# Six plain norms of the joined feed-forward and projection stage on Pool, with the pieces of the stage in another order

## The chip, the cores and the metric

One core of a Trainium2 chip runs the whole kernel as one program. TensorE multiplies and transposes (PE in the profile), VectorE is DVE, ScalarE is ACT, GpSimd is Pool (POOL); SyncE (SP) starts the DMAs. Each engine works through its own list of instructions in order, and they meet only at semaphores. The metric is the time of one execution on the device in microseconds (us), as the median of several runs; lower is better.

## The reference, cut to what matters

```python
x = x + _L0_xattn_ref(_layernorm(x), ctx_512, ctx_512, ...)   # 16 heads, keys and values from ctx_512
x = x + _L0_ffn_ref(_layernorm(x), w_gate, w_up, w_down)      # ternary feed-forward, 8-bit activations
x = x + _L1_xattn_ref(_layernorm(x), ctx_512, ...)            # LN, self-attention + FF, LN, cross-attention + FF
x = x + _L1_ffn_ref(_layernorm(x), W1, W2, Wg, bg)            # one of 8 experts per token

def _bitlinear(x, w):                  # the ternary layers
    return jnp.einsum('bsi,oi->bso', _act_quant(x), _weight_quant(w))
gate = jax.nn.silu(_bitlinear(x, w_gate)); up = _bitlinear(x, w_up)
return _bitlinear(gate * up, w_down)

# L1: x = _ln(xx, ln1_g, ln1_b); then q, k, v from _ln(x, ...) for 16 heads of 32, S = 256, width 256
```

x has the shape (8, 256, 256), f32. `_act_quant` scales each row by its largest absolute value to 127 and rounds. "Plain" norm means (x - mean) / sqrt(var + eps) without gain and bias.

## The kernel before, in words

The 2048 rows of x are cut into 16 tiles of 128 rows; NP = 4 "pairs" p of 4 tiles each (512 rows) are the unit in which most pieces work, X[p] holds a pair, Y[p] the input of the second block. The program has six stages: first cross-attention ("L0", to about 135 us), the joined stage (to about 306 us), self-attention a1, its feed-forward, cross-attention a2, experts.

The joined stage does two things for each pair, one pair behind the other. First the ternary feed-forward: `attended_sum` adds the attention's output to X[p]; `front_stats` (bn_stats, bn_aggr), then `front_apply` writes the plain norm of X[p] to XHB; `front_scales` and `front_quant` quantize it to N1 (bf16 integers) and `input_transposes`/`input_copy` turn it into N1T. For each tile i of the pair, `gate_up(p, i, j)` multiplies by half j of both weights, `silu` (ScalarE) and `gated` (VectorE) form the hidden row tile HH, `hidden_quant` quantizes it, `whole` (ScalarE) makes bf16 integers, `hidden_transposes`, `whole_copy`, `down` and `down_sum` bring the result into X[p]. Then the input of the second attention: `output_stats`, `gain` and `bias` (a norm with gain and bias, to Y[p]), `normed_stats`, and `second_norm` writes the plain norm of Y[p] to XHC; `a1_transposes`, `a1_input(p, "x")` and `a1_input(p, "y")` (ScalarE) and 12 pieces `project(p, k)` with `project_copy` follow, four each for queries, keys and values.

The reciprocal roots of all norms are made by Pool: `rstd` waits for the variance (`var_ready`), adds eps, takes the power -0.5 and signals `rstd_ready`. The statistics lie in a ring of four places in `small`, and Pool takes them strictly in the order in which VectorE makes them. In the joined stage Pool has nothing else.

The order of the pieces is written out by hand, one call after the other, for each of VectorE, ScalarE and TensorE. A piece waits by semaphore for what it needs. Between neighbours that matter here: `gate_up` of tile g waits for `gated` of tile g-1, half j (the PSUM bank); `hidden_transposes` of tile g for `whole_copy` of tile g-1; `down` of g for `down_sum` of g-1; `a1_transposes(p)` for the norm in XHC and for the 12th `project_copy` of the pair before; `gain(p)` writes into XHC and waits for the transposes of pair p-1; `a1_transposes(0)` also waits for `attended_sum(3)`.

In lines of the profile: L714 `apply` (all plain norms on VectorE), L871 the largest value in `quant_scales`, L878 `attended_sum`, L896 and L898 `front_quant`, L905 `gated`, L913 `hidden_quant`, L917 `down_sum`, L698 and L701 statistics, L722 `gain`, L729 `bias`; TensorE: L1648 transposes of f32 rows, L1904 `input_transposes`, L1915 `gate_up`, L1931 `hidden_transposes`, L1940 `down`, L2003 and L2005 `project`; ScalarE: L1356 `input_copy`, L1364 `silu`, L1369 `whole`, L1376 `whole_copy`, L1382 `a1_input`, L1395 `project_copy`; Pool: L488 to L492 `rstd`.

Of the kernel before, what the change touches and what calls it, by code (L numbers as in the profile page):

```python
# [48 lines left out]
def build(nc, ins, out):  # L49
    ctx = ExitStack()  # L50
    with ctx:
# [239 lines left out]
        def first_weights(b):  # L291
# [75 lines left out]
        with nc.Block() as block:  # L367
# [125 lines left out]


# [189 lines left out]
            def _(dve):  # L684
# [266 lines left out]
                kf1 = front_stats(1)  # L951
# [6 lines left out]
                hidden_quant(0, 0)  # L958
# [49 lines left out]
                gated(2, 2, 0)
                bias(1, ko1)
                gated(2, 2, 1)  # L1010
                kn1 = normed_stats(1)
                hidden_quant(2, 2)
                second_norm(1, kn1)
# [1421 lines left out]
```

## Time and profile before

| | before |
|---|---|
| runs | 1103.16 us median (1101.93 to 1103.17, 3 runs) |
| the execution under the profile | 1102.89 us, span 1101.1 us |
| TensorE matmuls busy | 1032.0 us, 94% of the span |
| VectorE busy | 535.5 us, 49% |
| ScalarE busy | 465.4 us, 42% |
| Pool busy | 268.5 us, 24% |
| mean granted TensorE clock | 0.994 of full |

Busy shares are of the whole span, and its stages have different limits, so a change in one stage is read from the stretch of that stage and from the waits in it. A row of the timeline gives the start, the length from the first start to the last end, the engine and line, the output and inputs, the count of instructions merged, and in brackets how long the engine was idle before it and what ended that.

### The profile page before, as it was taken

What the parts mean: (1) busy time and instruction counts of PE and PEld (TensorE: products, weight loads), DVE (VectorE), ACT (ScalarE), POOL (GpSimd) and SP (SyncE); (2) the same over time, 40 slices, a digit from 0 to 9 for tenths busy, and PEclk for the clock granted to TensorE, in tenths of its full rate; (3) what the DMA queues carried; (4) which work ended last, traced back from release to release, by engine and by line L of the source; (5) the groups of instructions that cost most, each with busy time, mean ns of one, the idle gap of its engine ahead of it and who ended that gap; (6) DMA issues with size and microseconds to landing.
All of it is one profiled execution on the core that took longest, in us unless ns stands there. A gap on an engine that the chain in (4) does not pass through costs nothing.

```text
span 1101.1 us, 20861 instructions
## 1 busy us (share of the span) xinstructions
PE 1032.0 (94%) x8679; PEld 740.4 (67%) x8679; DVE 535.5 (49%) x1293; ACT 465.4 (42%) x715; POOL 268.5 (24%) x409
## 2 busy tenths in 40 slices
PE   7998877999989999999999999999999999999997
PEld 4655544555467777776676475667578658999996
DVE  5577789985257788741531333775332233200000
ACT  6767565665455555552222325554311231122220
POOL 3023201101023334332212111556320102322211
PEclk9999999999999999999999999999999999999999
DMA  8600000000060000000000020000710217755410
GB/s 256 90 2 1 2 1 1 1 1 0 1 153 2 2 3 2 2 1 1 1 1 0 1 96 1 3 2 2 229 39 21 95 46 271 282 190 189 161 51 1
DMA packets 55359, 60.56 MB, mean 55 GB/s; under 512 B 23603, under 2 KB 47071, under 8 KB 55266
## 3 DMA queue, kind: packets, MB, share of 16 engines
q1 hardware_dynamic: 52322, 52.93, 15.7%
q0 software_dynamic: 2944, 6.30, 1.9%
q8 instruction: 69, 1.13, 0.4%
q14 instruction: 24, 0.20, 0.1%
HBM read 54.76 MB, written 7.21 MB: 56 GB/s over the span
## 4 chain that ended last, share of the span: by engine, by line
PE 72%; DVE 19%; ACT 3%; issue 2%; DMA 1%; POOL 1%; SPq 1%; DVEq 0%; POOLq 0%; ACTq 0%
PE ps L1879 15%; PE ps L2179 10%; DVE small L790 9%; PE ps L2321 8%; PE ps L2334 7%; PE ps L1739 6%; PE ps L2003 3%; PE ps L1710 3%; PE ps L2254 3%; PE ps L1792 2%; PE ps L1730 2%; PE ps L1707 2%; PE ps L1648 2%; PE ps L2005 1%; DVE small L871 1%
## 5 line engine op out<-in xcount | busy, mean ns | idle before, releaser
L790 DVE TENSOR_REDUCE small<-ps 128x4 f32<-128x1024 f32 (+2 forms) x112 | 145.4, 1334 | 74.8 <-PE ps L1710 60.0
L1879 PE MATMUL ps<-r_w,r_k 128*128 128x256 f32 x512 | 113.2, 381 | 2.5 <-ACT r_k L1549 2.5
L2179 PE MATMUL ps<-r_a,r_w 128*128 128x512 f32 x256 | 112.1, 594 | 3.1 <-ACT r_a L1382 3.1
L1879 PEld LDWEIGHTS ps<-r_w,r_k 128*128 128x128 f32 x512 | 96.4, 190 | 18.6 <-issue 4.4
L1792 PE MATMUL ps<-r_a,onesf 128*32 128x256 f32 (+1 forms) x768 | 84.3, 387 | 8.3 <-ACT r_a L1302 8.3
L2179 PEld LDWEIGHTS ps<-r_a,r_w 128*128 128x128 f32 x256 | 48.2, 190 | 60.2 <-issue 56.0
L2321 PE MATMUL ps<-r_a,w_block 128*128 128x128 f32 x736 | 86.4, 275 | 1.0 <-ACT r_a L1610 1.0
L2321 PEld LDWEIGHTS ps<-r_a,w_block 128*128 128x128 f32 x736 | 85.6, 192 | 2.5 <-ACT r_a L1610 1.0
L1549 ACT ACTIVATE r_k<-ps,pvec 128x512 f32<-128x512 f32 x64 | 44.0, 687 | 100.6 <-PE ps L2179 100.6
L1302 ACT ACTIVATE r_a<-ps 120x1024 f32<-120x1024 f32 (+1 forms) x64 | 65.5, 1024 | 43.5 <-PE ps L1746 43.2
L2334 PE MATMUL ps<-w_all,r_a 128*128 x368 | 83.2, 379 | 0.2 <-issue 0.2
L1618 ACT ACTIVATE r_a<-ps 128x512 f32<-128x512 f32 x46 | 27.5, 597 | 129.3 <-PE ps L2321 115.8
L578 POOL TENSOR_SCALAR_AFFINE_SELECT r_a<-r_a 128x256 f32<-128x256 f32 x128 | 47.5, 407 | 120.8 <-ACT r_a L1302 120.8
L1313 ACT ACTIVATE r_a<-ps 128x512 f32<-128x512 f32 (+1 forms) x64 | 45.0, 704 | 69.9 <-PE ps L1799 50.0
L2334 PEld LDWEIGHTS ps<-w_all,r_a 128*128 128x128 f32 x368 | 68.2, 190 | 8.7 <-issue 0.3
L1305 ACT ACTIVATE r_a<-ps 120x512 f32<-120x512 f32 (+1 forms) x128 | 69.4, 596 | 6.4 <-PE ps L1746 6.4
L1746 PE MATMUL ps<-maxT,sel 32*120 32x256 f32 (+1 forms) x512 | 65.2, 363 | 2.4 <-ACT maxT L1295 2.4
L491 POOL TENSOR_TENSOR small<-small,epst 128x4 f32<-128x4 f32 (+2 forms) x31 | 6.2, 199 | 224.8 <-DVE small L701 224.5
L2003 PE MATMUL ps<-r_a,r_w 128*128 128x512 f32 x128 | 58.7, 597 | 1.5 <-issue 0.9
L1382 ACT ACTIVATE r_a<-ps,pvec 128x512 f32<-128x512 f32 x40 | 28.6, 775 | 71.3 <-PE ps L1648 66.7
L1879 PE MATMUL ps<-r_w,r_q 128*128 128x256 f32 x256 | 57.0, 380 | 0.1
L1792 PEld LDWEIGHTS ps<-r_a,onesf 128*32 128x32 f32 (+1 forms) x768 | 31.2, 108 | 32.1 <-ACT r_a L1302 14.6
(265 smaller groups left out, 1816.7 us busy)
## 6 DMA issues: line engine op xcount, KB each, us to landing
w_block<-in_L_ffn_W SPq DMA_DIRECT2D x23, 1024.0 KB
w_all<-in_L_ffn_W SPq DMA_DIRECT2D x8, 1024.0 KB, 9.4
r_w<-in_L_xattn_a_li_w SPq DMA_DIRECT2D x4, 1024.0 KB, 7.3
x_rows<-x_all SPq DMA_DIRECT2D x4, 512.0 KB, 3.0
x_rows<-r_a SPq DMA_DIRECT2D x4, 512.0 KB, 3.0
x_all<-in_x SPq DMA_DIRECT2D x3, 512.0 KB, 5.8
y_all<-in_L_ffn_w_gate SPq DMA_DIRECT2D x1, 1024.0 KB, 8.8
y_all<-in_L_ffn_w_up SPq DMA_DIRECT2D x1, 1024.0 KB, 11.3
```

The lines of the kernel that those rows point to most:

```text
L578: ins_ = pool.affine_select(out=PM[:, 2 * h:2 * h + 2, x, :], in_=PT[:, 2 * h:2 * h + 2, q0:q0 + P], compare_op=ALU.is_gt, fill=0.0, base= ...
L790: ins_ = dve.tensor_reduce(nm.rearrange("p (j s) -> p j s", j=4)[:, j:j + count, :], src, AX.X, ALU.max, negate=True)
L1302: act.activation(PT[0:nk, 0:2, :], bank(n % 2, 0, 2)[0:nk], ACT.Exp, scale=scale).then_inc(sem["exp_done"], 1)
L1305: act.activation(PT[0:nk, 2:4, S * x:S * (x + 1)], bank(n % 2, 2, 2)[0:nk, :, S * x:S * (x + 1)], ACT.Exp, scale=scale).then_inc(sem["exp_ ...
L1739: pe.matmul(bank(n % 2, j)[0:nk, column(None, x)], keys(n, j, x), queries(n, j, x), start=(x == 0), stop=False, tile_position=(32 * j, 0))
L1746: ins_ = pe.matmul(bank(n % 2, j)[0:nk, column(None, x)], sel[32 * j:32 * j + 32, 0 if UNIT_OF[n][0] == "a1" else x, 0:nk], maxT[32 * j:32 ...
L1792: pe.matmul(bank(n % 2, 1)[32 * j:32 * j + 32, at:at + S], ones, weights_of(n, j, x), start=(a == "a2" or x == 0), stop=(a == "a2" or x == ...
L1879: ins_ = pe.matmul(o[:, t // 2, (t % 2) * D:(t % 2 + 1) * D], src[:, c, t * P:(t + 1) * P], w[:, c, :], start=(c == 0), stop=(c == chunks ...
L2003: ins_ = pe.matmul(o, w[:, c, m * P:(m + 1) * P], x[:, c, :], start=(c == 0), stop=(c == KC - 1))
L2179: ins_ = pe.matmul(o, LI[a]["li2"][:, c, m * P:(m + 1) * P], FT3[:, c, :], start=(c == 0), stop=(c == KC - 1))
L2321: ins_ = pe.matmul(ps[:, 2 * (b % 2) + h, m * P:(m + 1) * P], W1B[w][:, c, (4 * h + m) * P:(4 * h + m + 1) * P], FB[b % 2][:, c, :], start ...
L2334: ins_ = pe.matmul(ps[:, 4 + b % 2, 0:D], HB[b % 2][:, c, :], W2A[:, bass.ds(e, 1), c, :].rearrange("p o n -> p (o n)"), start=(c == 0), s ...
```

## The change

Six applications of a plain norm move from VectorE to Pool: `front_apply` for pairs 1, 2 and 3 and `second_norm` for pairs 0, 1 and 2. `front_apply(0)` and `second_norm(3)` stay on VectorE. Pool's new code (new lines, with the roots around it):

```diff
+                def normalise(dst, src):
+                    at = LN_W * ((norms - 1) % 4)
+                    pool.wait_ge(sem["rstd_ready"], norms)
+                    for t in range(PT_TILES):
+                        ins_ = pool.tensor_scalar(dst[:, t, :], src[:, t, :], sa(at + 48 + 2 * t, 1), sa(at + 72 + t, 1), ALU.subtract, ALU.mult)
+                    return ins_
+                def front_apply(p):
+                    pool.wait_ge(sem["n1_ready"], p)
+                    normalise(XHB, X[p]).then_inc(sem["front_ready"], 1)
+                def second_norm(p):
+                    normalise(XHC, Y[p]).then_inc(sem["c_xh_ready"], 1)
...
                 rstd()
+                front_apply(1)
                 rstd()
+                front_apply(2)
                 rstd(twice=True)
                 rstd()
+                second_norm(0)
                 rstd()
+                front_apply(3)
                 rstd(twice=True)
                 rstd()
+                second_norm(1)
                 rstd(twice=True)
                 rstd()
+                second_norm(2)
...
                 def front_scales(p):
+                    if p >= 1:
+                        dve.wait_ge(sem["front_ready"], p)
...
-                gated(0, 0, 0)
-                front_apply(1, kf1)
+                hidden_quant(0, 0)
                 front_scales(1)
```

The rest is the order of the calls, on VectorE, ScalarE and TensorE. `hidden_quant` of tile (0, 0) comes before the feed-forward scales of pair 1; `attended_sum(3)` comes behind `normed_stats(0)` and `hidden_quant(1, 1)`; `front_scales(3)` and `front_quant(3)` come before `output_stats(1)`. On TensorE each `hidden_transposes` and `down` of the middle of the stage stands somewhat earlier among the gate_up and project pieces, `input_transposes(1)` stands before `down(0, 1)`, and at the end the first scores of a1 come before `project(3, 4)` and `project(3, 5)` and not behind them. On ScalarE a `whole` is moved in between `a1_input(0, "x")` and `a1_input(0, "y")`, and `whole(3, 2)` stands earlier among the project copies, further ahead of `a1_input(2, "x")`. Nothing is computed otherwise and no DMA moves.

VectorE, from the gain of pair 0 to the first `hidden_quant` behind it. Before (L878 is `attended_sum(3)`, the two L714 are `second_norm(0)` and `front_apply(2)`):

```order
L722 SCALAR_TENSOR_TENSOR r_a<-x_all,small,bvec 128x256 x4
L905 SCALAR_TENSOR_TENSOR r_a<-ps,small,r_a 128x512
L729 SCALAR_TENSOR_TENSOR y_all<-r_a,small,bvec 128x256 x4
L905 SCALAR_TENSOR_TENSOR r_a<-ps,small,r_a 128x512
L698 BN_STATS small<-y_all 128x6 x4
L701 BN_AGGR small<-small 128x2 x4
L878 TENSOR_TENSOR x_all<-ps,x_all 128x1024
L714 TENSOR_SCALAR r_a<-y_all,small 128x256 x4
L905 SCALAR_TENSOR_TENSOR r_a<-ps,small,r_a 128x512
L714 TENSOR_SCALAR r_a<-x_all,small 128x256 x4
L871 TENSOR_REDUCE small<-r_a 128x1
```

The same place on VectorE afterwards (lines are about 22 to 24 higher: L744 is gain, L751 bias, L929 gated, L893 to L937 `hidden_quant`, L900 `attended_sum(3)`):

```order
L744 SCALAR_TENSOR_TENSOR r_a<-x_all,small,bvec 128x256 x4
L751 SCALAR_TENSOR_TENSOR y_all<-r_a,small,bvec 128x256 x4
L929 SCALAR_TENSOR_TENSOR r_a<-ps,small,r_a 128x512
L720 BN_STATS small<-y_all 128x6 x4
L723 BN_AGGR small<-small 128x2 x4
L893 TENSOR_REDUCE small<-r_a 128x1
L894 TENSOR_SCALAR small<-small 128x1
L895 RECIPROCAL small<-small 128x1
L936 TENSOR_SCALAR small<-small,mean_w 128x1
L937 TENSOR_SCALAR r_a<-r_a,small 128x1024
L900 TENSOR_TENSOR x_all<-ps,x_all 128x1024
L929 SCALAR_TENSOR_TENSOR r_a<-ps,small,r_a 128x512 x2
```

Both norms are gone from VectorE, one gated half-tile has moved behind, and `hidden_quant(1, 1)` has moved ahead of `attended_sum(3)`.

TensorE around the first a1 transposes. Before (L1879 is `output(3)`, L1648 the a1 transposes of pair 0, L2003 `project(0, 0)`):

```order
L1879 MATMUL ps<-r_w,r_v 128x256 x8
L1915 MATMUL ps<-r_k,r_a 128x512 x16
L1931 MATMUL ps<-identb,r_a 128x128 x8
L1648 MATMUL ps<-ident,r_a 128x128 x8
L1915 MATMUL ps<-r_k,r_a 128x512 x4
L1940 MATMUL ps<-r_v,r_a 128x256 x8
L2003 MATMUL ps<-r_a,r_w 128x512 x2
```

TensorE at the same place afterwards (L1897 `output(3)`, L1958 `down`, L1933 `gate_up`, L1949 `hidden_transposes`, L1666 a1 transposes, L2021 `project(0, 0)`):

```order
L1897 MATMUL ps<-r_w,r_v 128x256 x8
L1958 MATMUL ps<-r_v,r_a 128x256 x8
L1933 MATMUL ps<-r_k,r_a 128x512 x4
L1949 MATMUL ps<-identb,r_a 128x128 x8
L1666 MATMUL ps<-ident,r_a 128x128 x8
L1933 MATMUL ps<-r_k,r_a 128x512 x8
L1958 MATMUL ps<-r_v,r_a 128x256 x8
L1949 MATMUL ps<-identb,r_a 128x128 x8
L2021 MATMUL ps<-r_a,r_w 128x512 x2
```

The hidden transposes right ahead of the a1 transposes are now those of tile (1, 1) and no longer of (1, 0), and one more down and one more hidden transpose stand ahead of `project(0, 0)`.

Pool from the root of `front_stats(2)` on, before:

```order
L491 TENSOR_TENSOR small<-small,epst 128x4
L492 TENSOR_TENSOR small<-small,neghalf 128x4
L488 TENSOR_TENSOR small<-small,onepe 128x4
L489 TENSOR_TENSOR small<-small,eps 128x4
L492 TENSOR_TENSOR small<-small,neghalf 128x4
```

Pool at the same place afterwards:

```order
L491 TENSOR_TENSOR small<-small,epst 128x4
L492 TENSOR_TENSOR small<-small,neghalf 128x4
L499 TENSOR_SCALAR r_a<-x_all,small 128x256 x4
L488 TENSOR_TENSOR small<-small,onepe 128x4
L489 TENSOR_TENSOR small<-small,eps 128x4
L492 TENSOR_TENSOR small<-small,neghalf 128x4
L491 TENSOR_TENSOR small<-small,epst 128x4
L492 TENSOR_TENSOR small<-small,neghalf 128x4
L499 TENSOR_SCALAR r_a<-y_all,small 128x256 x4
```

Each moved norm stands right behind the root that it uses and ahead of the next root.

## Rows read from the trace of the kernel before

**Rows 1.** Stretches: busy us (instructions) of the five engines, granted clock, DMA share, GB/s.
```profile
174.00:186.00 12.00, 7.12 (x37) 4.25 (x36) 11.61 (x30) 5.64 (x10) 1.21 (x2) 0.86 0.00 1
...
139.00:225.00 86.00, 72.00 (x403) 42.17 (x402) 81.92 (x204) 52.83 (x71) 8.05 (x15) 0.96 0.00 1
225.00:306.00 81.00, 79.68 (x293) 38.50 (x290) 40.12 (x100) 41.85 (x64) 5.69 (x10) 1.00 0.00 1
```

**Rows 2.** Timeline of TensorE, 140 to 306 us: start, length, work, idle before.
```profile
180.57 1.97 PE L1648 MATMUL ps<-ident,r_a 128*128 128x128 f32 x8 [3.02 <-DVE r_a L714]
...
185.50 1.96 PE L2003 MATMUL ps<-r_a,r_w 128*128 128x512 f32 x4 [0.53 <-ACT r_a L1382]
...
191.23 0.61 PE L1931 MATMUL ps<-identb,r_a 128*128 128x128 bf16 x8
191.68 1.04 PE L1940 MATMUL ps<-r_v,r_a 128*128 128x256 bf16 x8
193.05 0.61 PE L1904 MATMUL ps<-identb,r_a 128*128 128x128 bf16 x8 [0.33 <-ACT r_a L1376]
...
220.08 1.07 PE L1648 MATMUL ps<-ident,r_a 128*128 128x128 f32 x8
...
223.72 0.62 PE L1904 MATMUL ps<-identb,r_a 128*128 128x128 bf16 x8 [0.84 <-DVE r_a L898]
...
254.18 1.07 PE L1648 MATMUL ps<-ident,r_a 128*128 128x128 f32 x8
...
259.39 7.11 PE L2003 MATMUL ps<-r_a,r_w 128*128 128x512 f32 x16 [0.93 <-issue]
...
281.16 1.09 PE L1648 MATMUL ps<-ident,r_a 128*128 128x128 f32 x8 [0.39 <-DVE r_a L714]
```

**Rows 3.** Timeline of VectorE in the joined stage.
```profile
139.92 1.37 DVE L714 TENSOR_SCALAR r_a<-x_all,small 128x256 f32<-128x256 f32 x4
...
145.25 1.21 DVE L871 TENSOR_REDUCE small<-r_a 128x1 f32<-128x1024 f32 x1
...
147.67 1.22 DVE L878 TENSOR_TENSOR x_all<-ps,x_all 128x1024 f32<-128x1024 f32 x1
...
159.59 0.48 DVE L917 SCALAR_TENSOR_TENSOR x_all<-ps,small,x_all 128x256 f32<-128x256 f32 x1 [1.06 <-PE ps L1940]
...
177.79 1.23 DVE L878 TENSOR_TENSOR x_all<-ps,x_all 128x1024 f32<-128x1024 f32 x1
...
180.43 0.74 DVE L905 SCALAR_TENSOR_TENSOR r_a<-ps,small,r_a 128x512 f32<-128x512 f32 x1
181.09 1.37 DVE L714 TENSOR_SCALAR r_a<-x_all,small 128x256 f32<-128x256 f32 x4
...
215.78 1.19 DVE L871 TENSOR_REDUCE small<-r_a 128x1 f32<-128x1024 f32 x1
...
219.87 1.21 DVE L871 TENSOR_REDUCE small<-r_a 128x4 f32<-128x1024 f32 x1
...
250.27 1.38 DVE L714 TENSOR_SCALAR r_a<-y_all,small 128x256 f32<-128x256 f32 x4 [1.40 <-POOL small L492]
```

**Rows 4.** Timeline of ScalarE in the joined stage.
```profile
139.91 0.69 ACT L1364 ACTIVATE r_a<-ps,small 128x512 f32<-128x512 f32 x1 [0.69 <-PE ps L1915]
...
172.90 1.14 ACT L1369 ACTIVATE r_a<-r_a,neg_magic 128x1024 bf16<-128x1024 f32 x1
...
182.58 2.78 ACT L1382 ACTIVATE r_a<-ps,pvec 128x512 f32<-128x512 f32 x4 [2.81 <-PE ps L1648]
```

**Rows 5.** Pool's groups by shape: busy us, mean ns, idle before.
```profile
L578 POOL TENSOR_SCALAR_AFFINE_SELECT r_a<-r_a 128x256 f32<-128x256 f32 x128 | 47.5, 407 | 120.8 <-ACT r_a L1302 120.8
...
L585 POOL TENSOR_TENSOR y_all<-y_all,bvec 128x256 f32<-128x256 f32 x32 | 23.9, 747 | 16.2 <-DVE max_rows L796 16.2
```

**Rows 6.** Timeline of all engines, 104 to 106 us.
```profile
104.76 1.19 DVE L868 TENSOR_SCALAR r_k<-r_k 128x2048 f32<-128x2048 f32 x1
104.92 1.62 POOL L542 TENSOR_TENSOR r_v<-r_a 128x256 f32<-128x256 f32 x1 [4.70 <-DVE r_a L820]
```

More of the change, by code:

```diff
@@ L978, in _ @@
                 gain(0, ko0)
+                bias(0, ko0)
                 gated(1, 1, 1)
-                bias(0, ko0)
+                normed_stats(0)
+                hidden_quant(1, 1)
+                attended_sum(3)
                 gated(1, 2, 0)
-                kn0 = normed_stats(0)
-                attended_sum(3)
-                second_norm(0, kn0)
                 gated(1, 2, 1)
-                front_apply(2, kf2)
-                hidden_quant(1, 1)
+                hidden_quant(1, 2)
                 down_sum(1, 0)
-                hidden_quant(1, 2)
                 front_scales(2)
@@ L995, in _ @@
                 hidden_quant(1, 3)
-                kf3 = front_stats(3)
                 gated(2, 0, 0)
+                front_stats(3)
                 gated(2, 0, 1)
-                front_apply(3, kf3)
+                gated(2, 1, 0)
                 hidden_quant(2, 0)
-                gated(2, 1, 0)
                 gated(2, 1, 1)
+                hidden_quant(2, 1)
                 down_sum(1, 2)
-                hidden_quant(2, 1)
+                front_scales(3)
+                gated(2, 2, 0)
+                front_quant(3)
+                gated(2, 2, 1)
                 down_sum(1, 3)
                 ko1 = output_stats(1)
+                hidden_quant(2, 2)
                 gain(1, ko1)
-                gated(2, 2, 0)
                 bias(1, ko1)
[L1010 to L1013, printed above, removed]
+                normed_stats(1)
                 down_sum(2, 0)
-                front_scales(3)
-                front_quant(3)
-                down_sum(2, 1)
                 gated(2, 3, 0)
@@ L1020, in _ @@
                 hidden_quant(2, 3)
-                down_sum(2, 2)
+                down_sum(2, 1)
                 gated(3, 0, 0)
                 gated(3, 0, 1)
+                down_sum(2, 2)
                 hidden_quant(3, 0)
-                down_sum(2, 3)
                 gated(3, 1, 0)
                 gated(3, 1, 1)
+                gated(3, 2, 0)
                 hidden_quant(3, 1)
+                down_sum(2, 3)
                 ko2 = output_stats(2)
-                gated(3, 2, 0)
+                gated(3, 2, 1)
                 gain(2, ko2)
+                hidden_quant(3, 2)
                 bias(2, ko2)
-                kn2 = normed_stats(2)
-                second_norm(2, kn2)
-                gated(3, 2, 1)
-                hidden_quant(3, 2)
+                normed_stats(2)
                 down_sum(3, 0)
@@ L2137, in _ @@
                 scores(FIRST["a1"])
+                project(3, 4)
+                project(3, 5)
                 project(3, 6)
```

165 lines of the change are left out of this document (81 added, 84 removed).

## The prediction

> **What bounds the kernel now.** The run under the profile took 1102.89 us around a span of 1101.1 us, so 1.8 us lie outside the span; the median of the runs is 1103.16 us, 0.27 us above the profiled run. I add up against 1102.89. A measurement of this kernel can tell about 0.2%, 2.2 us, from no change.
>
> I looked first at the busy time by stretch. The edit reaches only the joined stage, about 135 to 306 us, and this stage has two halves with different limits [rows 1]. From 139 to 225 us VectorE is busy 81.9 of 86 us and TensorE 72.0. From 225 to 306 us TensorE is busy 79.7 of 81 us and VectorE 40.1. So VectorE sets the pace first and TensorE afterwards. Work taken off VectorE counts only in the first half, and only if TensorE has something to do with the time.
>
> Then the timeline of TensorE with the idle time before each piece, to see what a gain can be made of [rows 2]: 3.02 us before the transposes of the first second-attention input at 180.57, 0.53 at 185.50, 0.33 at 193.05, 0.84 at 223.72, 0.93 at 259.39, 0.39 at 281.16. The second half has almost nothing to win: from 225 us on it is a queue of matmuls, and it ends when they are done. The stage gets shorter by as much idle (and slow) TensorE time as goes away, not by as much as VectorE is relieved.
>
> There is slow time too: in the stretch 174 to 186 us the granted clock is 0.86 on average [rows 1]. The f32 transposes at 180.57, after 3.02 us of idle, take 1.97 us, the same eight at 281.16 take 1.09 [rows 2]. A long wait costs TensorE nearly 1 us again behind it.
>
> **The change, part by part.**
>
> *Off VectorE.* Six norms of four instructions. The row at 139.92 is 1.37 us, the last at 250.27 is 1.38 [rows 3], so 6 x 1.37 = 8.2 us. The last of the six stands where TensorE is the limit and hides its absence: 5 x 1.37 = 6.9 us is all that VectorE can give, and an upper end for the gain from this part.
>
> *Onto Pool.* 24 instructions that subtract and multiply, 128x256. No row shows that on Pool. The nearest from below is the one-input select of the same size, 0.41 us; from above the two-input add, 0.75 us [rows 5]. The new one reads one big input as the select does, so I take 0.45 to 0.5 each, 2.0 us for four, with 1.6 to 3.0 as the bounds. On VectorE it was 1.37 us, so the result of a norm comes later than before, counted from its statistics: 1.40 us for the root on Pool (the wait of VectorE before 250.27 [rows 3]) plus 2.0 instead of 1.4.
> The three norms of the feed-forward input have slack: norm 1 is ready at about 141 and is wanted only after hidden_quant(0, 0), at about 143.7; norms 2 and 3 are ready long before. I cost them at nothing, hidden by hidden_quant and its neighbours. The three for the second attention are not hidden: a1_transposes waits for them.
> The same Pool queue holds every reciprocal root. Behind front_apply(2) stands the root of output_stats(0), some 6 us later; no root comes within 2 us of a moved norm.
>
> *The first half, rewalked.* hidden_quant takes 147.67 - 145.25 = 2.42 us from start to start; one half-tile of gated takes 181.09 - 180.43 = 0.66 [rows 3]. In the old order the sum attended_sum(3) starts at 177.79. In the new one front_apply(1) is gone (-1.4, start to start), gated(1, 2, 0) stands behind (-0.66), hidden_quant(1, 1) ahead of it (+2.42). gated(0, 0, 1) finds its ScalarE piece (139.91 to 140.60 [rows 4]) unready and waits some 0.7 us that front_apply(1) used to cover; of the 1.06 us wait at 159.59 [rows 3] about 0.6 goes, since quantization 1 is earlier but down(0, 1) now stands behind input_transposes(1). Sum: 177.8 - 1.4 - 0.7 + 2.4 + 0.7 - 0.6 = 178.2 us.
> TensorE now has hidden_transposes(1, 1) in front of the a1 transposes. They need hidden_quant(1, 1), done at 178.3, and ScalarE's copy of it, 1.14 us [rows 4]: 179.5 us. So TensorE idles longer than before, about 4.5 us (from 175 on), and runs slowly again: the hidden transposes some 0.9 us, twice their 0.45 (below), the a1 transposes from 180.4 with 1.97 us, to 182.4. At full clock it would be 180.0 and 181.1. Then ScalarE makes both inputs (2.78 us, row 182.58) with one whole copy of 1.14 between them [rows 4], 3.9 us: project(0, 0) starts between 185.0 and 186.3; I take 186.1. Before it is 185.50 [rows 2], so **0.6 us is lost** here. But by then three more pieces are done than before: down(1, 1), hidden_transposes(1, 1) and hidden_transposes(1, 2). Start to start a hidden transpose is 191.68 - 191.23 = 0.45 us, a down 193.05 - 0.33 - 191.68 = 1.04 [rows 2]; I take 0.9 for the down, since its end overlaps the next piece. That is 1.8 us of work. **Ahead by 1.2 us.**
>
> *From there on.* VectorE has no second_norm and front_apply any more, and front_scales(3) and front_quant(3) stand before output_stats(1), so N1 for input 3 is there long before TensorE asks. The waits of 0.33 and 0.84 us go. The 0.93 us before 259.39 is project(2, 0) waiting for ScalarE's inputs [rows 2]; whole(3, 2) no longer stands before those on ScalarE, so it goes too. **+2.1 us.**
> Is Pool on time here? For norm 1, VectorE needed 215.78 - 177.79 = 38.0 us from attended_sum(3) to the end of normed_stats(1). Now three norms are missing there (-4.1), gated(1, 2, 0) is in (+0.7), front_scales(3) and front_quant(3) are in (+3.8, from 219.87 [rows 3] to the transposes released at 223.72 [rows 2]): 178.2 + 38.0 + 0.4 = 216.6. XHC is there at 216.6 + 1.4 + 2.0 = 220.0. TensorE took 220.08 - 185.50 = 34.6 us from project(0, 0) to a1_transposes(1) [rows 2]; now gate_up(2, 3, 1) and input_transposes(3) come before it, 0.9 + 0.5, two hidden transposes and the 0.33 wait are gone, -1.2: 186.1 + 34.8 = 220.9. On time with 0.9 us of slack. For norm 2, gate_up(3, 2, 1) ends at about 238.5, and gated, gain, hidden_quant(3, 2), bias and statistics follow it on VectorE, 0.7 + 1.7 + 2.4 + 1.7 + 1.8 = 8.3: 246.8, with a wait for ScalarE 247.5; XHC at 250.9. TensorE's place is 254.18 [rows 2] less what is gained by then, 1.2 + 0.33 + 0.84: 251.8, slack 0.9 again. These slacks are of the size of my errors, so I take off **0.3 us** for them. The last norm stays on VectorE, and its 0.39 us wait stays.
>
> *The scores before project(3, 4).* Nothing: max_transposes stands behind project(3, 11) either way, and what follows it waits for ScalarE's last project_copy and the table load behind that.
>
> Sum: 1.2 + 2.1 - 0.3 = 3.0 us. 1102.89 - 3.0 = **1099.9 us**.
>
> **A row and a rule that speak against it.** Pool and VectorE disturb each other in this trace. Pool's multiply at 104.92 took 1.62 us, where the add of the same size takes 0.75, and VectorE's one-input 128x2048 instruction ran from 104.76 for 1.19 us [rows 5, 6]: 0.9 us lost by Pool. A moved norm meets about one such VectorE instruction, the scaling in hidden_quant, shorter than that one: an estimated loss of up to 0.7 us, within the slack of each norm that TensorE waits for.
> The Trainium skill, "SBUF — State Buffer", section "Who interferes with whom", says that the port pair shared by VectorE and GpSimd is an exclusive lock, and that whoever issues second is blocked for the whole instruction. By that VectorE would lose too, when Pool is first. The row shows only Pool's loss; no row before shows VectorE's.
>
> **The rivals.**
> 1. *VectorE is held up by Pool.* Each of the five norms of the first half makes VectorE wait once or twice for one Pool instruction of 0.45 us, 2.3 to 4.5 us in the half where VectorE is the limit. For it: VectorE is 95% busy there, so hardly a Pool instruction runs beside idle. Against: most of what VectorE does is reductions, statistics and PSUM reads, and its one disturbed neighbour in the trace was Pool. At 2.3 us the gain is 0.7 us: 1102.2.
> 2. *Pool is too slow, and the a1 transposes wait for it: slower.* With x us more per norm than the 2.0 assumed, the first transposes are late by x - 1.2 (XHC at 178.2 - 2.4 + 1.4 + 2.0 = 179.2 against 180.4), the other two by x - 0.9 each. At 0.75 a piece (x = 1.0) that is 0.2, still 1100.1. The whole gain is gone at 3x - 3.0 = 3.0, x = 2.0 or 1.0 us a piece, and it is slower by 0.2% from x = 2.7, 1.18 us a piece. At 1.3 (x = 3.2) 6.6 us are lost: 1106.5. For it: the 1.62 us row. Against: that row is one in several, and 24 pieces would have to be hit.
> 3. *The order is better than my walk.* If TensorE does not slow down after its wait and Pool is on time, the 0.6 loss and the 0.3 go and about 1 us of slow time too: gain 4.9, 1098.0.
> 4. *Nothing of it reaches the end*: the norms move as said, but the chain down, statistics, gain, bias, norm, transposes, ScalarE inputs sets project(0, 0) and then a1 transposes 1 to 3, as it did; 1102.9.
>
> **How the numbers follow.** The forecast with its own range, 1098.6 to 1101.6, has 0.54; rival 1 0.14, rival 2 0.12, rival 3 0.11, rival 4 0.09. Of the forecast's 0.54 some 0.42 lies above a gain of 2.2 us. Faster: 0.42 + 0.11 = 0.53. Slower: 0.09 of rival 2, and 0.04 from rival 1 at its upper end and from a chain that I misread, 0.13. Same: the rest, 0.34. The range goes from rival 3 with a little more, 1097.4, over rivals 1 and 4 and the milder half of rival 2, to 1104.0.
>
> **What the profile after would show.** Pool: 24 new instructions at 0.4 to 0.55 us; more than 0.9 is rival 2. VectorE: the 128x1024 scaling in hidden_quant and the 128x256 in front_quant keep the same duration everywhere; if some are 0.4 us longer, rival 1. TensorE: an idle of 4 to 5 us before the hidden transposes at about 179 us, project(0, 0) at 185 to 186.5, hardly any idle from there to the a1 transposes of pair 3, and those at about 278 instead of 281.16. After 306 us everything is the same and only earlier. I would be wrong if TensorE idles again between 186 and 250 us, which would mean that VectorE or ScalarE is late where I found slack of only 1 to 2 us (gate_up(2, 1, 1), down(1, 3)).

## The result, and the profile after

| | before | after |
|---|---|---|
| median of the runs | 1103.16 us (1101.93 to 1103.58, 6 runs) | 1109.31 us (1107.04 to 1111.48, 6 runs) |
| the execution under the profile | 1102.89 us, span 1101.1 | 1111.48 us, span 1109.8 |
| TensorE matmuls busy | 1032.0 us | 1038.7 us |
| VectorE busy | 535.5 us | 527.9 us |
| Pool busy | 268.5 us | 298.8 us |

The ratio is 1.0052, 95% interval 1.004 to 1.0064: slower by 6 us (0.5%) where 3 us less was forecast. The profiled execution is the longest of the six, so the trace shows 8.7 us of span where the medians show 6.2.

First, where the time is. The stretch from 139 us to the first transposes of the a1 maxima (305.78 before, 314.50 after), and the rest; columns as in [rows 1]. Before:

```profile
139.00:305.78 166.78, 151.46 (x692) 80.53 (x691) 122.04 (x304) 94.65 (x132) 13.74 (x25) 0.98 0.00 1
305.78:1100.00 794.22, 761.25 (x6621) 581.12 (x6619) 323.15 (x791) 278.41 (x449) 219.34 (x319) 1.00 0.20 64
```

After, with the stretch of the first a1 transposes on top:

```profile
174.00:186.00 12.00, 5.33 (x31) 3.72 (x31) 11.69 (x27) 2.86 (x3) 6.16 (x6) 0.73 0.00 1
...
139.00:314.50 175.50, 157.05 (x693) 84.54 (x691) 114.62 (x280) 95.94 (x132) 43.97 (x49) 0.93 0.00 1
314.50:1109.00 794.50, 761.20 (x6621) 581.07 (x6619) 323.04 (x791) 278.41 (x449) 219.67 (x319) 1.00 0.20 64
```

Behind the stage both kernels have the same busy times. In it the same matmuls (692 and 693 records) take 8.7 us more: 5.6 us more busy time of TensorE, since the mean granted clock is 0.93 and not 0.98, and 3.1 us more idle (175.50 - 157.05 = 18.45 against 15.32). Some 1 us of the slow time lies at the very start, ahead of any wait for Pool: from 139 to 143 us the clock is 0.62 after and 0.94 before. That need not come from the change: e1 and e7 below, which keep TensorE's old order, have 0.68 and 0.55 there. VectorE has 7.4 us less to do and nothing comes of it.

The timeline of TensorE after, at the places of [rows 2]:

```profile
181.35 1.04 PE L1949 MATMUL ps<-identb,r_a 128*128 128x128 bf16 x8 [4.43 <-ACT r_a L1387]
184.02 1.97 PE L1666 MATMUL ps<-ident,r_a 128*128 128x128 f32 x8 [1.64 <-POOL r_a L499]
185.79 3.62 PE L1933 MATMUL ps<-r_k,r_a 128*128 128x512 bf16 x8
...
190.84 1.94 PE L2021 MATMUL ps<-r_a,r_w 128*128 128x512 f32 x4
192.61 0.61 PE L1922 MATMUL ps<-identb,r_a 128*128 128x128 bf16 x8
...
194.83 1.89 PE L1933 MATMUL ps<-r_k,r_a 128*128 128x512 bf16 x8
...
228.36 1.97 PE L1666 MATMUL ps<-ident,r_a 128*128 128x128 f32 x8 [2.98 <-POOL r_a L499]
230.12 1.91 PE L1958 MATMUL ps<-r_v,r_a 128*128 128x256 bf16 x8
...
264.13 1.09 PE L1666 MATMUL ps<-ident,r_a 128*128 128x128 f32 x8 [1.80 <-POOL r_a L499]
...
268.14 7.11 PE L2021 MATMUL ps<-r_a,r_w 128*128 128x512 f32 x16
...
289.88 1.09 PE L1666 MATMUL ps<-ident,r_a 128*128 128x128 f32 x8 [0.42 <-DVE r_a L736]
```

Each of the three a1 transposes whose norm went to Pool now ends a wait for Pool: 1.64, 2.98 and 1.80 us, 6.4 together. Behind the first two TensorE runs near the lower of its two clocks, 1.2 of 2.4 GHz (granted 0.54 from 181 to 190.5 us and 0.56 from 228 to 235): eight gate_up matmuls at 185.79 take 3.62 us, eight of the same at 194.83 take 1.89. The waits of 0.33, 0.84 and 0.93 of [rows 2] are gone (192.61 and 268.14 have none). The last a1 transposes stand at 289.88, not 281.16; this start is the mark that I compare below. A mark is from one execution, and executions scatter: those of the kernel before lie between 1101.5 and 1106.3 us, and e1, whose time equals that kernel's and whose only edit lies on Pool, has the mark at 282.32. I take a difference of less than about 1 us at the mark as not shown.

Pool's norms, first in the timeline and then as groups (busy us, mean ns of one):

```profile
139.54 4.86 POOL L499 TENSOR_SCALAR r_a<-x_all,small 128x256 f32<-128x256 f32 x4 [0.20 <-POOL small L492]
...
179.02 4.95 POOL L499 TENSOR_SCALAR r_a<-y_all,small 128x256 f32<-128x256 f32 x4
...
223.04 5.26 POOL L499 TENSOR_SCALAR r_a<-y_all,small 128x256 f32<-128x256 f32 x4
...
259.24 4.84 POOL L499 TENSOR_SCALAR r_a<-y_all,small 128x256 f32<-128x256 f32 x4
```

```profile
L499 POOL TENSOR_SCALAR r_a<-x_all,small 128x256 f32<-128x256 f32 x12 | 15.2, 1275 | 0.5 <-POOL small L492 0.5
L499 POOL TENSOR_SCALAR r_a<-y_all,small 128x256 f32<-128x256 f32 x12 | 15.1, 1267 | 0.3
```

1.27 us a piece, where the forecast took 0.45 to 0.5.

### The profile page after: what moved, and what is told of

It is laid out like the page before. It is cut to its first block, busy times and chain, and to the rows that moved or that the text cites. A ratio compares the mean times of both kernels' runs of the same rounds, so it can differ in the third digit from the quotient of the medians.

```text
span 1109.8 us, 20862 instructions
## 1 busy us (share of the span) xinstructions
PE 1038.7 (94%) x8679; PEld 744.9 (67%) x8679; DVE 527.9 (48%) x1269; ACT 466.2 (42%) x715; POOL 298.8 (27%) x433
## 4 chain that ended last, share of the span: by engine, by line
PE 72%; DVE 18%; ACT 3%; POOL 3%; issue 2%; DMA 1%; SPq 1%; DVEq 0%; POOLq 0%; ACTq 0%
PE ps L1897 15%; PE ps L2197 10%; DVE small L812 9%; PE ps L2339 7%; PE ps L2352 7%; PE ps L1757 6%; PE ps L1728 3%; PE ps L2021 3%; PE ps L2272 2%; PE ps L1810 2%; PE ps L1748 2%; PE ps L1666 2%; PE ps L1725 2%; PE ps L1933 1%; POOL r_a L499 1%
## 5 line engine op out<-in xcount | busy, mean ns | idle before, releaser
L1897 PE MATMUL ps<-r_w,r_k 128*128 128x256 f32 x512 | 113.2, 381 | 2.5 <-ACT r_k L1567 2.5
L1897 PEld LDWEIGHTS ps<-r_w,r_k 128*128 128x128 f32 x512 | 96.4, 190 | 18.6 <-issue 4.4
L2021 PE MATMUL ps<-r_a,r_w 128*128 128x512 f32 x128 | 57.8, 596 | 0.0
L1897 PE MATMUL ps<-r_w,r_q 128*128 128x256 f32 x256 | 57.1, 380 | 0.1
```

The source lines that it names most:

```text
L1897: ins_ = pe.matmul(o[:, t // 2, (t % 2) * D:(t % 2 + 1) * D], src[:, c, t * P:(t + 1) * P], w[:, c, :], start=(c == 0), stop=(c == chunks ...
L2021: ins_ = pe.matmul(o, w[:, c, m * P:(m + 1) * P], x[:, c, :], start=(c == 0), stop=(c == KC - 1))
```

## The experiments

Three theories stood at the start. P: the form of Pool's instruction is dear in itself, and what follows is lateness at the a1 transposes. L: Pool and VectorE lock each other out, which makes both slow. O: the new order of the pieces is worse, whoever makes the norms. "The mark" is the start of the a1 transposes of pair 3.

| kernel | order | feed-forward norms 1 to 3 | second norms 0 to 2 | median us | ratio to before (95%) | mark |
|---|---|---|---|---|---|---|
| before | old | VectorE | VectorE | 1103.2 to 1103.7 | 1 | 281.16 |
| after | new | Pool | Pool | 1109.3 | 1.0052 (1.004, 1.0064) | 289.88 |
| e2_cheap | new | left out | left out | 1102.0 | 0.9985 (0.9975, 0.9994) | 279.77 |
| e3_order_only | new | VectorE | VectorE | 1106.5 | 1.0027 (1.0018, 1.0037) | 286.18 |
| e4_norms_only | old | Pool | Pool | 1115.3 | 1.0102 (1.0085, 1.0119) | 293.51 |
| e5_fronts_pool | new | Pool | VectorE | 1103.9 | 1.0002 (0.9993, 1.0011) | 282.43 |
| e8_split | new | Pool | 2 tiles each | 1105.6 | 1.0019 (1.001, 1.0028) | 283.45 |
| e6_double_second | new | Pool | Pool, twice | 1127.3 | 1.0216 (1.0201, 1.0232) | 308.02 |
| e7_old_fronts23 | old | 2, 3 on Pool | VectorE | 1102.8 | 0.9998 (0.9989, 1.0007) | 280.76 |
| e9_hybrid_cheap | old, then new | left out | left out | 1105.0 | 1.0007 (0.9998, 1.0015) | 282.61 |
| e10_hybrid_fronts | old, then new | 2, 3 on Pool | VectorE | 1107.2 | 1.0028 (1.0019, 1.0038) | 285.14 |
| e11_swap | new, one place changed | Pool | VectorE | 1103.4 | 1.0004 (0.9994, 1.0013) | 281.97 |

### e1: what a piece costs on Pool

Before, with instructions on Pool added behind the root at 139 us that write to unused space (twelve, where the expectation says 14; the last three repeat the second to the fourth):

```diff
+ pool.tensor_scalar(po[:, 0, :], bvec[:, 1, :], m_, r_, ALU.subtract, ALU.mult)
+ pool.tensor_scalar(po[:, 1, :], bvec[:, 1, :], m_, None, ALU.subtract)
+ pool.tensor_scalar(po[:, 2, :], bvec[:, 1, :], 0.5, 2.0, ALU.subtract, ALU.mult)
+ pool.tensor_scalar(po[:, 3, :], bvec[:, 1, :], 0.5, None, ALU.subtract)
+ pool.tensor_copy(po[:, 4, :], bvec[:, 1, :])
+ pool.tensor_tensor(po[:, 5, :], bvec[:, 1, :], m_.to_broadcast([P, D]), ALU.subtract)
+ link(pool.tensor_scalar(po[:, 6:8, :], bvec[:, 1:3, :], m_, r_, ALU.subtract, ALU.mult))
+ link(pool.tensor_scalar(po[:, 0:4, :], bvec[:, 1:5, :], m_, r_, ALU.subtract, ALU.mult))
+ pool.tensor_scalar(po[:, 0, :], bvec[:, 1, :], m_, r_, ALU.subtract, ALU.mult)
...
```

> The old kernel with 14 extra Pool instructions in the 24 us in which Pool is idle after the first root of the joined stage; their results are used by nobody. They are the norm's own form (two per-partition scalars) at 256, 512 and 1024 elements, the same with one per-partition scalar, with two constants, with one constant, a copy, and a two-input subtract with a broadcast. Theory P (the form is dear on Pool): the norm's form takes about 1.2 us at 256 elements, every time, and grows in proportion (2.4 at 512, 4.8 at 1024), and one of the other forms is much cheaper. Theory L (the form is cheap, but Pool is locked out by VectorE): its shortest instance is near 0.5 us and the instances scatter. Which of P's causes it is (per-partition scalars or two operations) shows in the variants: with constants about 0.5 if the scalars are the cause, with one scalar about 0.7 if it is the number of operations. The kernel's time should stay within 1 us of before.

The kernel took 1103.22 us. Timeline of its Pool, in the order of the edit:

```profile
139.30 1.24 POOL L564 TENSOR_SCALAR r_a<-bvec,small 128x256 f32<-128x256 f32 x1
140.54 0.92 POOL L565 TENSOR_SCALAR r_a<-bvec,small 128x256 f32<-128x256 f32 x1
141.44 1.14 POOL L566 TENSOR_SCALAR r_a<-bvec 128x256 f32<-128x256 f32 x1
142.55 0.85 POOL L567 TENSOR_SCALAR r_a<-bvec 128x256 f32<-128x256 f32 x1
143.35 0.39 POOL L568 COPY r_a<-bvec 128x256 f32<-128x256 f32 x1
143.73 0.61 POOL L569 TENSOR_TENSOR r_a<-bvec,small 128x256 f32<-128x256 f32 x1
144.34 2.07 POOL L570 TENSOR_SCALAR r_a<-bvec,small 128x512 f32<-128x512 f32 x1
146.51 3.78 POOL L571 TENSOR_SCALAR r_a<-bvec,small 128x1024 f32<-128x1024 f32 x1
150.39 1.22 POOL L572 TENSOR_SCALAR r_a<-bvec,small 128x256 f32<-128x256 f32 x1
151.59 1.26 POOL L573 TENSOR_SCALAR r_a<-bvec,small 128x256 f32<-128x256 f32 x1
```

VectorE in the same stretch:

```profile
139.92 0.75 DVE L919 SCALAR_TENSOR_TENSOR r_a<-ps,small,r_a 128x512 f32<-128x512 f32 x1 [1.99 <-ACT r_a L1378]
140.58 1.74 DVE L728 TENSOR_SCALAR r_a<-x_all,small 128x256 f32<-128x256 f32 x4
```

The form itself costs 1.22 to 1.24 us. With constants for the two operands it is 1.14, with one operation and a constant 0.85, while a copy of the same size takes 0.39 and a subtraction with two inputs 0.61. From 512 to 1024 elements 1.71 us are added, 3.3 ns an element, less than the proportion that was expected (2.07 us at 512, where 2.4 was expected). The piece at 139.30 took 1.24 us although VectorE was idle until 139.92, and at 150.39, beside other work of VectorE, it is 1.22 again, so P holds for the price. What is left of L is small and goes both ways. VectorE's norm at 140.58, beside three of these, took 1.74 us where it takes 1.37 in [rows 3]. And the form with one operation and its operand from SBUF took 0.92 us at 140.54 but 1.26 at 151.59, where VectorE's scaling in hidden_quant (151.78, 0.82 us instead of 0.74) ran beside it.

### e2 to e4: the price, the order and the norms apart

e2 leaves the six norms out: a copying select stands in their place, 0.41 to 0.44 us a piece, and the order and all signals are those of after.

```diff
- ins_ = pool.tensor_scalar(dst[:, t, :], src[:, t, :], sa(at + 48 + 2 * t, 1), sa(at + 72 + t, 1), ALU.subtract, ALU.mult)
+ ins_ = pool.affine_select(out=dst[:, t, :], in_=src[:, t, :], compare_op=ALU.is_ge, fill=0.0, base=1, pattern=[[0, D]], channel_multiplier=0)
```

> The changed kernel with Pool's 24 norm instructions replaced by a copying select of the same size, which the trace shows at 0.41 us: the six norms are left out, the data go through unnormalised, order and waits are as in the change. Theory P (only Pool's price for the norm makes the change slow): the three waits before the a1 transposes (1.64, 2.98, 1.80 us) go, and the time is what I forecast with 1.6 to 2.0 us a norm, 1099.9, say 1098.5 to 1101.5. Theory O (the new order of the pieces is itself worse, with its longer TensorE wait at 176 to 181 us and the slow clock behind it): the time stays at 1105 or above.

e3 has the new order with all norms on VectorE, e4 the old order with the six norms on Pool.

In e3, against after, two places on VectorE; Pool's calls are gone and the other four norms come back alike.

```diff
- front_stats(1)
+ kf1 = front_stats(1)
  gated(0, 0, 0)
+ front_apply(1, kf1)
...
- normed_stats(0)
+ kn0 = normed_stats(0)
  hidden_quant(1, 1)
+ second_norm(0, kn0)
  attended_sum(3)
```

> The new order of the pieces on all engines, with all norms on VectorE: front_apply(1) between the two halves of gated(0, 0), front_apply(2) and (3) right before their front_scales, second_norm(0) behind hidden_quant(1, 1), second_norm(1) behind gated(2, 3), second_norm(2) behind its statistics. Theory P: VectorE gets its 6.9 us back in the first half, the a1 transposes wait for it and not for Pool: near the old kernel, 1101 to 1104. Theory O: 1107 or above, as the changed kernel.

> The old order of the pieces with the six norms on Pool as in the change. Theory P: front_scales(1) stands right behind gated(0, 0) and waits for Pool until about 144.5 instead of starting at 142.0, 2.4 us that were hidden in the new order; and each of the three a1 transposes waits 3 to 4 us for 4.9 us of norm. 1109 to 1113, no better than the changed kernel. Theory O: 1101 to 1104.

Measured: 1102.0, 1106.5 and 1115.3 us. Timeline of TensorE in e2; no piece of it waits for Pool:

```profile
181.49 1.03 PE L1949 MATMUL ps<-identb,r_a 128*128 128x128 bf16 x8 [4.27 <-ACT r_a L1387]
...
188.23 1.96 PE L2021 MATMUL ps<-r_a,r_w 128*128 128x512 f32 x4
...
279.77 1.09 PE L1666 MATMUL ps<-ident,r_a 128*128 128x128 f32 x8 [0.40 <-DVE r_a L736]
```

Four of these copies take 1.46 us together, a little less than the 2.0 that the forecast assumed. They are done 1.1, 0.7 and 1.6 us before TensorE begins the three a1 transposes (at 182.31, 222.37 and 254.07), so 2.0 us would have been in time too. With Pool cheap, then, the change wins 1.5 us (the forecast said 3.0). The expectation, 1098.5 to 1101.5, was missed by half a microsecond, since even with a cheap Pool the change wins less than was forecast. Between the medians of e2 and after lie 7.3 us, and they are the price: the length of 24 instructions on an engine that is 27% busy. Between the two profiled executions the mark moves by 10.1 us, 6.4 of them the waits for Pool and nearly all the rest slower matmuls behind them; the execution after is 2.2 us above its median and that of e2 0.7 below its own.

e3, the same view:

```profile
192.73 0.62 PE L1920 MATMUL ps<-identb,r_a 128*128 128x128 bf16 x8 [0.96 <-DVE r_a L914]
...
228.70 1.60 PE L1956 MATMUL ps<-r_v,r_a 128*128 128x256 bf16 x8 [1.81 <-DVE x_all L933]
```

The new order alone costs 3 us: with the norms on VectorE, front_quant(2) and down_sum come too late for it. It was made for a VectorE without norms. At 1106.5 e3 lies between what P (1101 to 1104) and O (1107 or above) had expected. e4, first VectorE where the feed-forward scales of pair 1 begin, then TensorE at the three a1 transposes:

```profile
144.17 1.22 DVE L894 TENSOR_REDUCE small<-r_a 128x4 f32<-128x1024 f32 x1 [2.57 <-POOL r_a L500]
...
188.42 1.97 PE L1667 MATMUL ps<-ident,r_a 128*128 128x128 f32 x8 [7.12 <-POOL r_a L500]
...
231.46 1.47 PE L1667 MATMUL ps<-ident,r_a 128*128 128x128 f32 x8 [2.82 <-POOL r_a L500]
...
267.71 1.10 PE L1667 MATMUL ps<-ident,r_a 128*128 128x128 f32 x8 [1.40 <-POOL r_a L500]
```

The old order has its a1 transposes right behind the norm, and there Pool's price costs even more, 7.12 us at the first. In this order a feed-forward norm is not free either: front_scales(1) waits 2.57 us for it, and the gate_up that stands at 173.70 before is at 177.46 here, 3.8 us late before any a1 transposes. The time is above the expected 1109 to 1113. Order and norms are no sum of parts: +3.0 alone, +11.9 alone, +6.2 together. O is true of the order alone, and not the cause in after.

### e5, e6 and e8: which norms, and how much

Theory W, after these: only the second norms are dear, because the a1 transposes ask for them at once. e5 gives them back to VectorE, e8 shares them two tiles to two, e6 has Pool make them twice.

```diff
  def second_norm(p):
+     link(normalise(XHC, Y[p]))
      normalise(XHC, Y[p]).then_inc(sem["c_xh_ready"], 1)
```

That is e6; in e8 Pool does tiles 0 and 1 and VectorE tiles 2 and 3:

```diff
- normalise(XHC, Y[p]).then_inc(sem["c_xh_ready"], 1)
+ normalise(XHC, Y[p], 2).then_inc(sem["c_xh_ready"], 1)
...
- apply(XHC, Y[p], k).then_inc(sem["c_xh_ready"], 1)
+ apply(XHC, Y[p], k, first=2 if p < 3 else 0).then_inc(sem["c_xh_ready"], 1)
```

> The changed kernel with its order, but only the three feed-forward norms (front_apply of pairs 1 to 3) on Pool; the three second norms are VectorE's again, behind hidden_quant(1, 1) and at the same places as in the order-only kernel. Theory W (only the second norms are dear, because a1 transposes and project wait for them at once, while a feed-forward norm has 5 us and more until front_scales asks for it): Pool's price of 1.22 us a piece is hidden for the fronts, the run stands between the kernel with the six norms left out (1102.0) and the new order with all norms on VectorE (1106.5), at 1102.5 to 1104.0, and no wait of TensorE for Pool is over 0.3 us. Rival F (Pool's long instructions cost wherever they stand, by VectorE's reads or by its rstd standing behind them): 1106 or more.

> The changed kernel with each of the three second norms on Pool done twice over (the second pass writes the same values), so each is ready some 4.9 us later. Theory W: the waits of TensorE at the a1 transposes grow from 1.64, 2.98 and 1.80 by 4.9 each and nothing takes it up, 1109.3 + 3 x 4.9 = about 1124, range 1121 to 1127, the upper end with a slower clock behind longer waits. Rival R (another chain ends the stage and Pool's lateness is partly parallel to it): 1113 to 1118.

> The changed kernel with each of the three second norms shared: tiles 0 and 1 on Pool (2.45 us), tiles 2 and 3 on VectorE (0.7 us), fronts on Pool as in the changed kernel. Theory W: a second norm is ready 2.4 us earlier, so the waits of 1.64 and 1.80 at the a1 transposes go and the one of 2.98 becomes about 0.5, while VectorE gives back 0.7 each time: 1109.3 - 5 = about 1104, range 1103 to 1105.5. Rival R (another chain sets the end there): above 1107.

Measured 1103.9 (e5, inside its range), 1127.3 (e6) and 1105.6 (e8): with 0, 2, 4 and 8 pieces of each second norm on Pool the medians are 1103.9, 1105.6, 1109.3, 1127.3. The second doubling costs 18.0 us. Pool in e6 at the first second norm, then TensorE:

```profile
179.44 10.78 POOL L499 TENSOR_SCALAR r_a<-y_all,small 128x256 f32<-128x256 f32 x8
...
190.27 1.97 PE L1667 MATMUL ps<-ident,r_a 128*128 128x128 f32 x8 [7.47 <-POOL r_a L499]
...
239.69 1.97 PE L1667 MATMUL ps<-ident,r_a 128*128 128x128 f32 x8 [7.92 <-POOL r_a L499]
...
279.70 1.97 PE L1667 MATMUL ps<-ident,r_a 128*128 128x128 f32 x8 [6.73 <-POOL r_a L499]
```

The eight instructions of the three norms take 10.78, 10.20 and 9.78 us, 15.7 us more than in after, and the three waits grew by just these 15.7 us: nothing else is on the path there. Now the third one too is followed by slow transposes, 1.97 us where after has 1.09 at 264.13. The expected upper end, 1127, was just passed. The feed-forward norms on Pool, at the same 1.27 us a piece, cost next to nothing in e5: no piece of TensorE waits for Pool in it, and VectorE waits 0.28 us for the first of them. Against e3 they are even worth 2.5 us.

e8 nearly fits too, 0.1 us above its range (1103 to 1105.5): one wait of 0.28 us for Pool is left of the three, but VectorE has 0.7 us more per pair, and down_sum is late:

```profile
224.55 1.10 PE L1669 MATMUL ps<-ident,r_a 128*128 128x128 f32 x8 [0.28 <-POOL r_a L499]
...
227.16 1.03 PE L1961 MATMUL ps<-r_v,r_a 128*128 128x256 bf16 x8 [1.52 <-DVE x_all L941]
```

### e7, e9, e10, e11: is a version left that wins

e7 keeps the old order and gives Pool only `front_apply` of pairs 2 and 3 (added behind their roots on Pool, taken from VectorE).

> The kernel before in its own order, with only front_apply of pairs 2 and 3 on Pool, right behind their roots; VectorE loses 8 pieces of 0.34 us. Theory W: Pool has more than 10 us until front_scales of either pair, so the norms are never late; VectorE is 1.37 us earlier at hidden_quant(1, 1) and at hidden_quant(2, 0), which takes away the 0.33 at 193.05 and part of the 0.84 and 0.93 later in the stage: 1101.5 to 1103.0 beside 1103.4 of before. Rival F: 1104 or more. If neither, no difference: 1103.4.

1102.8 us, ratio 0.9998: no difference, though the number lies in the expected 1101.5 to 1103.0. The waits before TensorE of [rows 2] are all there, 3.02, 0.52, 0.33, 0.84 and 0.94. The expectation that the later ones go was wrong: taking 2.7 us off VectorE does not bring forward what ends them.

e9 and e10 take the old order up to hidden_quant(1, 3), project_copy(0, 3) and gate_up(2, 0, 1), and the new one from there, e9 with the norms left out as in e2.

> The kernel with the six norms on Pool replaced by short copies (a copying select of 0.41 us a piece; the six norms are left out, the output is not the reference's), and the order of before up to hidden_quant(1, 3), project_copy(0, 3) and gate_up(2, 0, 1), the new order from there. Theory A (the new order loses in its first half, by hidden_quant(1, 1) ahead of attended_sum(3), hidden_transposes(1, 1) ahead of the a1 transposes and a TensorE idle for 4.3 us at a stretch, and gains in its second half): the a1 transposes of pair 3 stand at 278.5 or earlier, the time is 0.8 to 2 us under the 1102.0 of the kernel with copies and the whole new order, so 1100.0 to 1101.2. Rival B (the first half of the new order is what gains, as the prediction had it with 1.2 us): 1103 or more.

> The same hybrid of the two orders with every norm computed: the feed-forward norms of pairs 2 and 3 on Pool, all others on VectorE. Theory A: first half as before (the a1 transposes of pair 0 at about 180.3), second half without the 0.84 and 0.93, but with the 1.26 of the kernel with only the fronts on Pool at 226 (down_sum behind second_norm(1)): 1101.5 to 1103. Rival B: 1104 or more. No difference from before: 1103.5.

1105.0 and 1107.2 us: both missed, on the side of the rival. But the trace shows why this does not prove the rival. TensorE in e9:

```profile
200.14 1.04 PE L1933 MATMUL ps<-r_k,r_a 128*128 128x512 bf16 x4 [1.32 <-DVE r_a L929]
...
206.91 1.03 PE L1958 MATMUL ps<-r_v,r_a 128*128 128x256 bf16 x8 [1.84 <-DVE x_all L941]
...
282.61 1.09 PE L1666 MATMUL ps<-ident,r_a 128*128 128x128 f32 x8 [0.39 <-DVE r_a L736]
```

Neither before nor e2 has waits of this length at 200 and 207: they come with the joint, where, as I read the two orders, the old one has already spent two project pieces that the new one uses as filling. Without these 3.2 us the mark would be at 279.4, against 279.77 in e2 and 281.16 before. That is arithmetic and not a run. It would give the first half of the new order a loss of some 0.3 us and the second half a gain of some 1.7, but 0.3 us is less than the mark scatters, so the loss is not shown. What remains is that nothing shows the 1.2 us that the forecast gave to the first half. e10 has about the same two waits (1.32 and 1.97) and 1.25 us more at 228.88, and is no version to keep.

e11 is e5 with one place changed: down_sum(2, 1) ahead of hidden_quant(2, 3), with two gate_up ahead of hidden_transposes(2, 3) and a1_input(1, "x") ahead of whole(2, 3).

> The kernel with the new order and only the feed-forward norms on Pool, changed at one place: down_sum(2, 1) ahead of hidden_quant(2, 3) on VectorE, the two gate_up of tile (3, 0) ahead of hidden_transposes(2, 3) on TensorE, and a1_input(1, x) ahead of whole(2, 3) on ScalarE. If the wait of 1.26 before down(2, 2) at 226 is on the path that ends the stage, it goes and all behind comes 1.2 earlier: the a1 transposes of pair 3 at 281.2 instead of 282.4, the time about 1.1 under the 1103.9 of that kernel, 1102.3 to 1103.2. If the work behind takes it up (the hidden row tile of (2, 3) is now late by 2.5), nothing is won: 1103.9.

1103.4 us, mark 281.97. The wait of 1.26 at 226 in e5 became two:

```profile
227.75 0.62 PE L1949 MATMUL ps<-identb,r_a 128*128 128x128 bf16 x8 [0.71 <-ACT r_a L1387]
...
229.13 1.96 PE L2021 MATMUL ps<-r_a,r_w 128*128 128x512 f32 x4 [0.76 <-issue]
```

The two add up to 1.47 us, so nothing was won here. The half microsecond at the mark is not the edit's: the hidden transposes ahead of the first a1 transposes already stand at 181.51 and not 181.98, long before the place that was changed, and from there to the mark both kernels take 100.5 us. The medians can't be told apart either. The wait did not go but moved, near the expectation's second case. No version here beats the kernel before with the whole reference computed; e7, e5 and e11 equal it.

## Why the prediction was wrong

The main step that failed is the price of a moved norm on Pool; a second, smaller one is the walk of the first half.

*What bounds the stage* was read rightly: everything behind 314.5 us is the same, and the 7.4 us taken off VectorE won nothing by themselves.

*The price on Pool is the step that failed.* The forecast had no row for a subtract-and-multiply on Pool and bounded it by the select (0.41) and the two-input add (0.75) of [rows 5], took 0.45 to 0.5 for "reads one big input as the select does", and kept 3.0 us for four as the upper end. It is 1.27 us, 4.84 to 5.26 us for the four of a second norm. The two rows bounded other operations, and the number of inputs turned out to be no guide: the subtraction with two inputs took 0.61 us, the one with one input 0.85 (e1). e2 has Pool about as cheap as assumed (1.46 us for four, not 2.0, with slack for the difference), and with that the change is 1.5 us faster, at 1102.0: inside the wide range, 1097.4 to 1104.0, but just above the forecast's own, 1098.6 to 1101.6.

*Slack and lateness at the a1 transposes* held up. Rival 2 put the loss at x - 1.2 and twice x - 0.9 for x us above 2.0. With 4.95, 5.26 and 4.84 that is 1.75 + 2.36 + 1.94 = 6.1 us; the waits are 6.4. Its total of some 1106 was still short of 1109.3, for two reasons: it started from a gain of 3.0 where e2 has 1.5, and it had no slow clock behind the waits, though the prediction had read just that in [rows 2] for the first wait. In the profiled execution that is most of the 5.6 us by which TensorE's busy time in the stage grew. Rival 2 had a chance of 0.12, and the stated range took in only its milder half: its own case at 1.3 us a piece gave 1106.5. The price at which it turns slower (1.18 us a piece) was less than the 1.62 row that stood in [rows 6] and was explained away.

*The feed-forward norms cost nothing*: right for the new order, at almost three times the price (e5), but by little. Norm 1 was to be ready at about 141 and is ready at 144.4, when `hidden_quant(0, 0)` is just ending; in e4, without that piece ahead, VectorE waits 2.57 us for it. The distance to the next root was less than said, 0.61 us of idle on Pool before the root at 171.50 and not 2, but still enough.

*The walk of the first half.* The TensorE wait was to be 4.5 us; it is 4.43 (e2: 4.27). It was to end at 179.5 and ends at 181.35 (181.49 in e2), since hidden_quant(1, 1) is done at 180.1 and not 178.3. Timeline of VectorE in e2:

```profile
168.51 0.48 DVE L941 SCALAR_TENSOR_TENSOR x_all<-ps,small,x_all 128x256 f32<-128x256 f32 x1 [0.29 <-PE ps L1958]
...
173.67 1.67 DVE L751 SCALAR_TENSOR_TENSOR y_all<-r_a,small,bvec 128x256 f32<-128x256 f32 x4 [0.58 <-POOL small L492]
```

The 1.4 us of the missing front_apply(1) did not arrive. Most of it is gone at once: gated(0, 0, 0) starts 0.8 us later than before (140.09 against 139.26, behind slower matmuls, which is the scatter named above), and gated(0, 0, 1) then waits 0.90 us for ScalarE. The down sum at 168.51 waits 0.29 us for TensorE, and output_stats(0) starts at 169.57 where it started at 169.31 before. Then `bias` waits 0.58 for its root, which a gated piece between gain and bias used to hide; that the new order had moved it away was overlooked. So `project(0, 0)` stands at 188.23 in e2, 2.7 us later than the 185.50 before and not 0.6; with the 1.8 us of work done ahead of it the half is up to 0.9 us behind (most of which may be the late start), where +1.2 was written. *The later waits* of 0.33, 0.84 and 0.93 went as said.

*Rival 1* (VectorE held up by Pool) is nearly nothing. The scaling in hidden_quant took 0.90 us at 144.05, 0.91 at 179.20, 0.90 at 202.25 and 0.95 at 225.07, each beside a norm on Pool, where it takes 0.74 undisturbed: 0.2 us a time, not the 0.45 and more of the rival. At 167.49, beside a norm of 5.35 us on Pool, it kept its 0.74. And idle of 3.46 us on VectorE before 192.67 shows that it is not what TensorE waits for there.

## What to carry to other kernels

An operation that no row of the trace shows on the engine it goes to may lie outside what other operations of the same size suggest; one added instruction that writes to unused space gives its price before anything is moved. Move to a slow engine what is asked for late (here the feed-forward norms, with `hidden_quant` ahead of their reader), not what the busiest engine waits for at once, and count behind each new wait of TensorE the slow matmuls that follow it. An order tuned to one split of the work is no gain for another: here it was worth -1.5 us with cheap norms on Pool and +3 us with all norms on VectorE.

## What the runs showed of the hardware

On Pool, operations of one tensor and one or two scalars were dearer than the two-input ones: for 128x256 f32 1.22 to 1.24 us (two operations) and 0.85 to 0.92 (one; 1.26 once, beside VectorE's scaling), against 0.61 for the two-input subtraction, 0.75 for the add of [rows 5] and 0.39 for a copy. With constants the second operation costs 0.2 to 0.3 us (1.14 and 1.07 against 0.85); operands from SBUF in place of constants add about 0.1. VectorE does the same instruction in about 0.34. The length grows by 3.3 ns an element (2.07 us at 512, 3.78 at 1024), against 4.9 for four of 256; but each tile has its own mean and root, so the norm can't be joined so.

The Trainium skill, "GPSIMD Engine Reference", section "4.1 Engine selection", says that one-input elementwise work is roughly at line rate on GpSimd and two-input work about half as fast as on VectorE. The copy of e1 (0.39 us against 0.61 for two inputs) goes that way. The subtract-and-multiply does not: with one input it took twice as long as the two-input subtraction, and over three times what VectorE takes.

Behind a wait of 1.80 us (264.13 in after) the f32 transposes took 1.09 us, their length at the full clock (2.4 GHz); behind 2.98 us, and behind 1.64 us that itself followed one of 4.43, they took 1.97 us, as at half of it (1.2 GHz), and the matmuls right behind them were slow as well. The length of a wait alone does not settle it. In two other executions the same transposes, behind as long a wait as the 3.02 us before, were fast or nearly so, in e10 and then e1:

```profile
182.40 1.09 PE L1666 MATMUL ps<-ident,r_a 128*128 128x128 f32 x8 [3.02 <-DVE r_a L732]
```

```profile
181.63 1.18 PE L1662 MATMUL ps<-ident,r_a 128*128 128x128 f32 x8 [3.03 <-DVE r_a L728]
```

In both the next four gate_up matmuls took 1.81 and 1.91 us where they take 1.04 at the full clock. The slow time came all the same, only one piece later.
